# Cross attention: row sums directly behind the product with V in steps 6 and 14, half a V projection ahead of them

## The chip, the core and the metric

The kernel runs on one core of a Trainium2 chip. The metric is the device time of one execution in microseconds (us). Engines, by the names that the profile uses: PE is TensorE (matmuls), PEld its weight loads, DVE is VectorE, ACT is ScalarE, POOL is GpSimd, SP the engine that issues most DMAs. All arithmetic is in 32 bits; an operand of a projection is split into a high and a low part, and a projection is three matmuls.

## The reference

A transformer block on 16 batches of 224 tokens of width 512, with 16 heads of 32, and a context of 750 tokens. The part that matters here is the cross attention:

```
q_c = _ln(x) @ W_qc + b_qc
kv_c = _ln(context) @ W_kvc + b_kvc
k_c, v_c = split(kv_c)                      # B x NH x S x hd
c_attn_w = softmax(einsum(q_c, k_c) * hd ** -0.5)
c_attn_out = einsum(c_attn_w, v_c)
x = x + c_attn_out @ W_cproj + b_cproj
```

Self-attention stands ahead of it, an MLP with gelu behind it. Every batch has the full context.

## The kernel before, in words

Three phases follow each other on all engines: self-attention, cross attention, MLP. The change touches the cross attention alone (`cross_phase`).

There each engine runs a program of its own with `body`, once for each batch b, and in it 16 **steps** h, one for each head. Semaphores alone tie the engines together; the order of the work on each engine is written out by hand. In a step the kernel

- computes the scores of head h+1 with the queries on the partitions (`score`, L1779: unit 0 one matmul of 500 columns, unit 1 one of 500, unit 2 two of 250, into three banks `sc_ps`), from which VectorE takes the row maxima (`row_max`, L1965 and L1967);
- computes the transposed scores of head h-6 (`score_t`, three times two matmuls of 224 columns, L1793, into two banks `tr_ps`), on which ScalarE takes the exponential into `prT` (`exps`, L2138). `score_t` for part c+1 of a head waits until the exponential of the part before the last is done, since there are two banks;
- fills in one or two pieces of the projections for the next batches, by the table `FILL`: `("k", g, half)` and `("v", t)` are twelve matmuls (L72 to L74), of which the first six go between `score_t` 0 and 1 and the last six behind score unit 0; `("c", t)` is four transposes of the normalised context (L1740). They take turns on two banks, even and odd, in the order of `ORDER`, and `bank_free` makes each wait until the last use of its bank is taken out: by ScalarE (`high`) for V, by VectorE (`low`) behind ScalarE for K and c;
- every fourth step, turns the row maxima of four heads (`turn_maxima`, L1767) into the even or odd bank. VectorE splits them (`split_maxima`, L2012 and L2014), and SP places them by DMA beside the queries.

Every fourth step (h = 2, 6, 10, 14) a group of four heads has all its probabilities. Then the product with V (`pv`, L1806, 24 matmuls, four at a time on 32 columns of the array each; the profile has two records for each) and the sums of the probabilities (`sums`, L1815, four matmuls in the same form, of what GpSimd added up in L2211, L2213 and L2215) go into the bank `or_ps`. VectorE inverts the sums (`invert`, L2019) and multiplies (`normalize`, L2025).

In steps 2 and 10 both come at the end of the step. In steps 6 and 14, named by `PV_EARLY`, `FILL` has no projection; there `pv` stands behind `score_t` 0, where otherwise half a projection stands, and `sums` come at the end of the step after, 7 or 15. `divided` gives the step in which VectorE inverts and multiplies: for those groups one step later than for the others. The last batch's groups (`MID_PARTS`, `END_PARTS`) are done piece by piece in another way.

## Time and profile before

| | |
|---|---|
| median of 3 runs | 2614.72 us (2613.72 to 2615.62) |
| the profiled execution | 2619.34 us |
| its span, first to last instruction | 2617.5 us |
| mean granted TensorE clock | 0.991 of full speed |
| busy: PE, DVE, POOL, ACT | 98%, 65%, 49%, 43% of the span |

The profile is of one execution. Its timeline lists instructions of an engine by start, in us from the span's start, with how long each group took; matmuls overlap, so that the distance of two starts and not the duration is what one costs. Like instructions in a row are merged, with their number behind an x. Idle time before an instruction and what ended it stand in brackets.

### The profile page before, as it was taken

Reading aid. Unit: us, or ns where it says so; the run is one execution under the profiler, and the core shown is the slowest. Engines: PE = TensorE matmul, PEld = TensorE weight load, DVE = VectorE, ACT = ScalarE, POOL = GpSimd, SP = SyncE. Lnnn points to the kernel's source line nnn. Section 1 sums busy time; section 2 is a strip of 40 time slices with the busy share of each in tenths; the row PEclk is TensorE's granted clock in tenths of the full one; section 3 lists DMA queues with packets and bytes.
Section 4 is the critical chain, followed back from the end, with each engine's and each line's share of the span. In section 5 each row is a group of like instructions: output and inputs, shape, how many; then the busy total and the mean of one; then the engine's idle time right before and its main releaser. Section 6 shows DMA issues by size and latency. Waiting matters only on the chain.

```text
span 2617.5 us, 50236 instructions
## 1 busy us (share of the span) xinstructions
PE 2578.0 (98%) x18696; PEld 2133.6 (82%) x18696; DVE 1694.1 (65%) x3399; ACT 1126.6 (43%) x2192; POOL 1275.6 (49%) x1426
## 2 busy tenths in 40 slices
PE   8999999999999999999999999999899999999999
PEld 6688888888788888888888888887678888888887
DVE  6677777777757777777777777776764444444442
ACT  4354454444535555555555555554552221212111
POOL 1445455454436777777777777775421121220230
PEclk9999999999899999999999999999899999999999
DMA  8454545555454444444444444434521111111110
GB/s 225 128 136 125 135 120 130 129 129 132 137 148 111 115 115 112 113 114 112 117 114 116 119 113 115 121 90 102 153 94 45 37 44 34 45 49 37 45 53 17
DMA packets 193045, 269.89 MB, mean 103 GB/s; under 512 B 34788, under 2 KB 112612, under 8 KB 192788
## 3 DMA queue, kind: packets, MB, share of 16 engines
q1 hardware_dynamic: 187116, 254.16, 36.9%
q0 software_dynamic: 3264, 7.92, 0.9%
q10 hardware_dynamic: 2424, 4.61, 0.7%
q8 instruction: 150, 2.46, 0.4%
q14 instruction: 91, 0.75, 0.1%
HBM read 111.11 MB, written 36.77 MB: 56 GB/s over the span
## 4 chain that ended last, share of the span: by engine, by line
PE 69%; DVE 1%; issue 0%; DMA 0%; ACT 0%; SPq 0%; DVEq 0%; ACTq 0%
PE late_tr_ps L1793 7%; PE late_sc_ps L1779 7%; PE late_or_ps L1806 5%; PE late_even_ps L72 5%; PE late_sc_ps L72 5%; PE late_even_ps L73 5%; PE late_even_ps L74 5%; PE late_sc_ps L74 5%; PE late_sc_ps L73 5%; PE late_odd_ps L72 3%; PE late_odd_ps L74 3%; PE late_odd_ps L73 3%; PE late_tr_ps L74 2%; PE late_tr_ps L72 2%; PE late_tr_ps L73 2%; PE late_odd_ps L1740 1%
## 5 line engine op out<-in xcount | busy, mean ns | idle before, releaser
L2138 ACT ACTIVATE cross_prT<-late_tr_ps 125x448 f32<-125x448 f32 x759 | 403.0, 544 | 273.5 <-PE late_tr_ps L1793 264.6
L1965 DVE TENSOR_REDUCE cross_parts<-late_sc_ps 112x1 f32<-112x500 f32 x512 | 335.5, 663 | 221.8 <-PE late_sc_ps L1779 220.7
L2211 POOL TENSOR_TENSOR cross_part<-cross_prT 125x448 f32<-125x448 f32 x232 | 271.2, 1169 | 214.6 <-ACT cross_prT L2138 176.9
L1295 POOL TENSOR_TENSOR self_psum<-self_prT 112x224 f32<-112x224 f32 x256 | 179.0, 699 | 328.3 <-ACT self_prT L1160 319.5
L1793 PE MATMUL late_tr_ps<-cross_qst,cross_kst 98*125 98x224 f32 x1536 | 309.5, 284 | 5.4 <-ACT cross_prT L2138 4.4
L1793 PEld LDWEIGHTS late_tr_ps<-cross_qst,cross_kst 98*125 98x125 f32 x1536 | 255.3, 188 | 55.8 <-ACT cross_prT L2138 16.5
L2613 ACT ACTIVATE mlp_hv<-late_sc_ps,mlp_b 128x512 f32<-128x512 f32 x112 | 77.0, 687 | 511.5 <-PE late_sc_ps L74 497.1
L2213 POOL TENSOR_TENSOR cross_part<-cross_part,cross_prT 125x448 f32<-125x448 f32 x232 | 268.5, 1157 | 18.2
L1779 PE MATMUL late_sc_ps<-cross_kst,cross_qst 96*112 96x500 f32 (+1 forms) x1024 | 262.2, 337 | 5.2 <-PEq L99 3.3
L2527 DVE CAST mlp_hT_h<-mlp_hv 128x512 fp32r<-128x512 f32 x112 | 55.9, 499 | 301.8 <-ACT mlp_hv L2613 301.8
L1160 ACT ACTIVATE self_prT<-self_st_ps 112x448 f32<-112x448 f32 x256 | 138.4, 541 | 167.6 <-PE self_st_ps L628 166.4
L1779 PEld LDWEIGHTS late_sc_ps<-cross_kst,cross_qst 96*112 96x112 f32 x1024 | 165.2, 179 | 20.1 <-issue 3.5
L908 DVE TENSOR_REDUCE self_nmax<-self_sc_ps 112x2 f32<-112x448 f32 x256 | 154.5, 614 | 33.3 <-PE self_sc_ps L599 33.2
L72 PE MATMUL late_sc_ps<-mlp_xT_l,mlp_w_h 128*128 128x512 f32 x448 | 175.8, 393 | 0.0
L74 PE MATMUL late_sc_ps<-mlp_xT_h,mlp_w_h 128*128 128x512 f32 x448 | 175.2, 391 | 0.0
L73 PE MATMUL late_sc_ps<-mlp_xT_h,mlp_w_l 128*128 128x512 f32 x448 | 175.0, 391 | 0.0
L1967 DVE TENSOR_REDUCE cross_parts<-late_sc_ps 112x2 f32<-112x500 f32 x256 | 170.2, 665 | 0.0
L2215 POOL TENSOR_TENSOR cross_psum<-cross_part 125x224 f32<-125x224 f32 x232 | 155.6, 671 | 18.2
L1806 PE MATMUL late_or_ps<-cross_prT,cross_vt 125*32 125x224 f32 x2784 | 143.7, 354 | 0.0
L72 PE MATMUL self_pj_ps<-self_xT_l,self_wqkv_h 128*128 128x224 f32 x512 | 140.6, 275 | 2.4 <-DVE self_wm_gates L1009 1.4
L74 PE MATMUL self_pj_ps<-self_xT_h,self_wqkv_h 128*128 128x224 f32 x512 | 140.6, 275 | 0.0
L73 PE MATMUL self_pj_ps<-self_xT_h,self_wqkv_l 128*128 128x224 f32 x512 | 140.3, 274 | 0.0
(343 smaller groups left out, 6870.9 us busy)
## 6 DMA issues: line engine op xcount, KB each, us to landing
cross_kst<-cross_nat_h SPq DMA_DIRECT2D x508, 93.8 KB, 2.2
cross_kst<-cross_nat_l SPq DMA_DIRECT2D x254, 93.8 KB, 2.2
cross_qst<-qc SPq DMA_DIRECT2D x192, 112.0 KB, 2.5
cross_c_in<-in_context SPq DMA_DIRECT2D x78, 224.0 KB
self_kst<-self_nat_h SPq DMA_DIRECT2D x128, 112.0 KB, 2.3
self_qst<-self_natq_h SPq DMA_DIRECT2D x128, 112.0 KB, 3.0
self_x_in<-in_x SPq DMA_DIRECT2D x16, 448.0 KB, 3.8
self_kst<-self_nat_l SPq DMA_DIRECT2D x64, 112.0 KB, 2.2
```

The costliest lines, as they stand in the source:

```text
L72: pe.matmul(out, lhs[0], rhs[1], start=first, stop=False)
L73: pe.matmul(out, lhs[1], rhs[0], start=False, stop=False)
L74: return pe.matmul(out, lhs[0], rhs[0], start=False, stop=last)
L1295: pool.tensor_tensor(psum[:, j], prT[:, j, 0], prT[:, j, 1], ALU.add).then_inc(p_summed, 1)
L1779: last = pe.matmul(sc_ps[u][0:QN, at:at + cn], qst[g][0:TERMS * HD, j, t * QN:(t + 1) * QN], kst[g][j][0:TERMS * HD, c0:c0 + cn], start=Tr ...
L1793: last = pe.matmul(bank(h, c)[0:SN, m * N:(m + 1) * N], kst[g][j][:, kt * SN:(kt + 1) * SN], qst[g][:, j, :], start=True, stop=True)
L1806: last = pe.matmul(or_ps[HD * j:HD * j + HD, 0:N], vt[b.par][:, kt, h * HD:h * HD + HD], prT[:, slot(h), kt], start=kt == 0, stop=kt == ST ...
L1965: dve.tensor_reduce(parts[:, g % 2, j, u, 0:1], sc_ps[u][0:QN, 0:SHALF[0]], AX_X, ALU.max, negate=True).then_inc(maxed, 1)
L1967: dve.tensor_reduce(parts[:, g % 2, j, :, 1], sc_ps[u][0:QN, 0:QT * SHALF[1]].rearrange("p (t k) -> p t k", t=QT), AX_X, ALU.max, negate=T ...
L2138: act.activation(probabilities(b, h)[:, 2 * c:2 * c + 2], bank(h, c)[0:SN, 0:2 * N].rearrange("p (k t) -> p k t", k=2), ACT.Exp).then_inc( ...
L2211: pool.tensor_tensor(part[:], prT[:, j, 0:2], prT[:, j, 2:4], ALU.add).then_inc(pre_summed, 1)
L2213: pool.tensor_tensor(part[:], part[:], prT[:, j, 4:6], ALU.add).then_inc(pre_summed, 1)
```

## The change

`HALF_EARLY` names steps 7 and 15. Their V projection's first half moves to the step before, behind score unit 0 (and a second half, of which these steps have none). `pv` leaves its early place and stands with `sums` at the end of steps 6 and 14, as in 2 and 10. `divided` treats all groups alike, so VectorE inverts and multiplies one step earlier for these. `PV_EARLY` is left to put the transposes `("c", 4)` at the start of step 14.

```diff
+    HALF_EARLY = {7: 6, 15: 14}
...
         for back in (lag - 1, lag):
             step = last_step(b, h - back)
-            if (step < NH and ((h - back) % NH not in PV_EARLY or step >= 0)) == (back == lag - 1):
+            if (step < NH) == (back == lag - 1):
                 found += late_group(b, h - back, att, prv)
...
                 for o, l in late(b, h, att, prv):
                     score_t(o, l, 0)
-                for o, g in late_group(b, h, att, prv) if h in PV_EARLY and steady else ():
-                    pv(o, g)
                 for f, o in fill_at(b, h, "c") if h in PV_EARLY else ():
                     fill_(o, f)
-                for f, o in fill_at(b, h, "kv"):
+                for f, o in fill_at(b, h, "kv") if h not in HALF_EARLY else ():
                     fill_(o, f, (0,))
...
                 for f, o in fill_at(b, h, "kv"):
                     fill_(o, f, (1,))
+                for f, o in fill_at(b, h + 1, "kv") if HALF_EARLY.get(h + 1) == h else ():
+                    fill_(o, f, (0,))
...
-                for o, g in late_group(b, h, att, prv) if h not in PV_EARLY and steady else ():
+                for o, g in late_group(b, h, att, prv) if steady else ():
                     pv(o, g)
                     sums(o, g)
-                for o, g in late_group(b, h - 1, att, prv) if h - 1 in PV_EARLY and steady else ():
-                    sums(o, g)
```

The code below the new line stands one line lower: L1793 is L1794 in the changed kernel, and so on.

TensorE in step 6, before (`tr_ps` is a pair of transposed scores, `sc_ps` scores, `or_ps` the product with V and the sums, `even_ps` and `odd_ps` the banks of the fills; the trio is the last two L1779 rows):

```order
L1793 MATMUL late_tr_ps<-cross_qst_70,cross_kst_68 125x224 x2
L1806 MATMUL late_or_ps<-cross_prT,cross_vt_76 32x224 x24
L1793 MATMUL late_tr_ps<-cross_qst_70,cross_kst_68 125x224 x2
L1779 MATMUL late_sc_ps<-cross_kst_69,cross_qst_71 112x500
L1793 MATMUL late_tr_ps<-cross_qst_70,cross_kst_68 125x224 x2
L1779 MATMUL late_sc_ps<-cross_kst_69,cross_qst_71 112x500
L1779 MATMUL late_sc_ps<-cross_kst_69,cross_qst_71 112x250 x2
L1793 MATMUL late_tr_ps<-cross_qst_70,cross_kst_68 125x224 x2
L72 MATMUL late_even_ps<-cross_wkv_l,cross_cT_h 125x512
```

With the change:

```order
L1794 MATMUL late_tr_ps<-cross_qst_70,cross_kst_68 125x224 x4
L1780 MATMUL late_sc_ps<-cross_kst_69,cross_qst_71 112x500
L72 MATMUL late_even_ps<-cross_wkv_l,cross_cT_h 125x512
...
L1794 MATMUL late_tr_ps<-cross_qst_70,cross_kst_68 125x224 x2
L1780 MATMUL late_sc_ps<-cross_kst_69,cross_qst_71 112x500
L1780 MATMUL late_sc_ps<-cross_kst_69,cross_qst_71 112x250 x2
L1807 MATMUL late_or_ps<-cross_prT,cross_vt_76 32x224 x24
L1816 MATMUL late_or_ps<-cross_psum,cross_ones 32x224 x4
L1794 MATMUL late_tr_ps<-cross_qst_70,cross_kst_68 125x224 x4
```

The product with V went from between the first two pairs to the end of the step, the sums came up behind it from the end of step 7, and six V matmuls (L72 to L74, twice) came up from step 7.

TensorE in step 14, from the transposes that end step 13, before:

```order
L1740 MATMUL late_even_ps<-shared_ident,cross_c_in 128x125 x4
L1793 MATMUL late_tr_ps<-cross_qst_14188,cross_kst_14186 125x224 x2
L1806 MATMUL late_or_ps<-cross_prT,cross_vt_76 32x224 x24
L1740 MATMUL late_odd_ps<-shared_ident,cross_c_in 128x125 x4
L1793 MATMUL late_tr_ps<-cross_qst_14188,cross_kst_14186 125x224 x2
L1779 MATMUL late_sc_ps<-cross_kst_14193,cross_qst_14189 112x500
L1793 MATMUL late_tr_ps<-cross_qst_14188,cross_kst_14186 125x224 x2
L1779 MATMUL late_sc_ps<-cross_kst_14193,cross_qst_14189 112x500
L1779 MATMUL late_sc_ps<-cross_kst_14193,cross_qst_14189 112x250 x2
```

With the change, up to the end of step 14:

```order
L1741 MATMUL late_even_ps<-shared_ident,cross_c_in 128x125 x4
L1794 MATMUL late_tr_ps<-cross_qst_14188,cross_kst_14186 125x224 x2
L1741 MATMUL late_odd_ps<-shared_ident,cross_c_in 128x125 x4
L1794 MATMUL late_tr_ps<-cross_qst_14188,cross_kst_14186 125x224 x2
L1780 MATMUL late_sc_ps<-cross_kst_14193,cross_qst_14189 112x500
L72 MATMUL late_even_ps<-cross_wkv_l,cross_cT_h 125x512
...
L1794 MATMUL late_tr_ps<-cross_qst_14188,cross_kst_14186 125x224 x2
L1780 MATMUL late_sc_ps<-cross_kst_14193,cross_qst_14189 112x500
L1780 MATMUL late_sc_ps<-cross_kst_14193,cross_qst_14189 112x250 x2
L1807 MATMUL late_or_ps<-cross_prT,cross_vt_76 32x224 x24
L1816 MATMUL late_or_ps<-cross_psum,cross_ones 32x224 x4
```

The transposes into `odd_ps` and the pair behind them stand directly behind the first pair, and six matmuls into `even_ps`, last written by the transposes that end step 13, come before the second-to-last pair.

VectorE at the end of step 7 and in step 8, before:

```order
L1965 TENSOR_REDUCE cross_parts<-late_sc_ps 112x1
L1967 TENSOR_REDUCE cross_parts<-late_sc_ps 112x2
L1929 BN_STATS cross_st<-cross_c_in 125x6
L1965 TENSOR_REDUCE cross_parts<-late_sc_ps 112x1 x2
L1967 TENSOR_REDUCE cross_parts<-late_sc_ps 112x2
L1958 SCALAR_TENSOR_TENSOR cross_nat_l<-late_odd_ps,shared_bkv,cross_nat_h 128x376
L2019 RECIPROCAL cross_rb<-late_or_ps 128x224
```

With the change:

```order
L1964 TENSOR_REDUCE cross_parts<-late_sc_ps 112x1
L1966 TENSOR_REDUCE cross_parts<-late_sc_ps 112x2
L2018 RECIPROCAL cross_rb<-late_or_ps 128x224
L1928 BN_STATS cross_st<-cross_c_in 125x6
L1964 TENSOR_REDUCE cross_parts<-late_sc_ps 112x1
L2024 TENSOR_TENSOR cross_ou<-late_or_ps,cross_rb 128x224
L1964 TENSOR_REDUCE cross_parts<-late_sc_ps 112x1
```

The reciprocal moved from behind the row maxima of step 8 and the low part of K to ahead of them.

## Rows read from the trace of the kernel before

**Rows 1.** Stretch: us; busy PE, PEld, DVE, ACT, POOL; PE clock, DMA share, GB/s.

```profile
1298.10:1368.80 70.70, 70.69 (x582) 59.50 (x581) 51.66 (x99) 38.81 (x75) 52.31 (x57) 1.00 0.44 115
```

**Rows 2.** Timeline of TensorE, step 2: start, duration, engine, line, operation, count.

```profile
1341.28 0.63 PE L1779 MATMUL late_sc_ps<-cross_kst,cross_qst 96*112 96x500 f32 x3
1341.83 2.48 PE L1806 MATMUL late_or_ps<-cross_prT,cross_vt 125*32 125x224 f32 x48
1344.13 0.56 PE L1815 MATMUL late_or_ps<-cross_psum,cross_ones 125*32 125x224 f32 x8
1344.62 0.48 PE L1793 MATMUL late_tr_ps<-cross_qst,cross_kst 98*125 98x224 f32 x2
```

**Rows 3.** Timeline of TensorE, steps 6 and 7.

```profile
1355.07 0.38 PE L1793 MATMUL late_tr_ps<-cross_qst,cross_kst 98*125 98x224 f32 x2
1355.41 2.48 PE L1806 MATMUL late_or_ps<-cross_prT,cross_vt 125*32 125x224 f32 x48
...
1358.58 0.62 PE L1779 MATMUL late_sc_ps<-cross_kst,cross_qst 96*112 96x500 f32 x3
1359.03 0.38 PE L1793 MATMUL late_tr_ps<-cross_qst,cross_kst 98*125 98x224 f32 x2
...
1362.48 0.26 PE L1767 MATMUL late_odd_ps<-shared_ident,cross_nmax 112*8 112x112 f32 x1
...
1362.80 0.62 PE L1779 MATMUL late_sc_ps<-cross_kst,cross_qst 96*112 96x500 f32 x3
1363.35 0.58 PE L1815 MATMUL late_or_ps<-cross_psum,cross_ones 125*32 125x224 f32 x8
1363.87 0.48 PE L1793 MATMUL late_tr_ps<-cross_qst,cross_kst 98*125 98x224 f32 x2
1364.18 0.34 PE L72 MATMUL late_odd_ps<-cross_cT_l,cross_wkv_h 128*128 128x376 f32 x1
```

**Rows 4.** Timeline of ScalarE and of GpSimd around step 6.

```profile
1354.81 0.55 ACT L2138 ACTIVATE cross_prT<-late_tr_ps 125x448 f32<-125x448 f32 x1 [0.92 <-PE late_tr_ps L1793]
...
1359.58 0.68 POOL L2215 TENSOR_TENSOR cross_psum<-cross_part 125x224 f32<-125x224 f32 x1
```

**Rows 5.** Timeline of TensorE, steps 14 and 15.

```profile
1321.48 0.46 PE L1793 MATMUL late_tr_ps<-cross_qst,cross_kst 98*125 98x224 f32 x2
1321.86 2.48 PE L1806 MATMUL late_or_ps<-cross_prT,cross_vt 125*32 125x224 f32 x48
1324.27 0.65 PE L1740 MATMUL late_odd_ps<-shared_ident,cross_c_in 125*128 125x125 f32 x4
1324.67 0.46 PE L1793 MATMUL late_tr_ps<-cross_qst,cross_kst 98*125 98x224 f32 x2
...
1325.41 0.61 PE L1779 MATMUL late_sc_ps<-cross_kst,cross_qst 96*112 96x500 f32 x3
1326.03 0.48 PE L1793 MATMUL late_tr_ps<-cross_qst,cross_kst 98*125 98x224 f32 x2
...
1331.40 0.46 PE L1793 MATMUL late_tr_ps<-cross_qst,cross_kst 98*125 98x224 f32 x2
```

**Rows 6.** Timelines of ScalarE and VectorE, steps 13, 14 and 0.

```profile
1321.30 0.58 ACT L2099 COPY cross_vt<-late_odd_ps 125x512 f32<-125x512 f32 x1
...
1325.43 0.55 ACT L2138 ACTIVATE cross_prT<-late_tr_ps 125x448 f32<-125x448 f32 x1
...
1322.39 0.68 DVE L1952 TENSOR_TENSOR cross_cT_l<-late_even_ps,cross_cT_h 128x500 fp32r<-128x500 f32 x1
...
1336.56 1.55 DVE L2019 RECIPROCAL cross_rb<-late_or_ps 128x224 f32<-128x224 f32 x1
```

**Rows 7.** Timelines of TensorE and VectorE, step 11.

```profile
1311.48 0.26 PE L1767 MATMUL late_odd_ps<-shared_ident,cross_nmax 112*8 112x112 f32 x1
...
1312.44 0.62 PE L1740 MATMUL late_odd_ps<-shared_ident,cross_c_in 125*128 125x125 f32 x4
...
1312.08 0.26 DVE L2014 TENSOR_TENSOR cross_mrow_l<-late_odd_ps,cross_mrow_h 8x112 fp32r<-8x112 f32 x1
```

## The prediction

> **What bounds the kernel now.** Read first the busy time by stretch. Over one batch of the cross attention (70.70 us, which repeats from batch to batch) TensorE is busy for 70.69 us at granted clock 1.00, the others for 52 us or less [rows 1]. So the time is the sum of TensorE's own queue, and the busy share hides two kinds of loss in it: a matmul that starts later than its form needs, because the kind of matmul changed, or because it waited for another engine for less than the one before takes to drain. Both show only in start-to-start times, so I read the timeline of TensorE next, and always subtract start from start. The durations printed there overlap; they are not the cost.
>
> Words used below: a pair is the two L1793 matmuls of one score_t; a single is the one 500-column L1779 matmul of a head, a trio the three that follow; turn is L1767; PV is L1806, sums is L1815; c is four L1740 transposes.
>
> **Prices of the pieces.** A trio takes 0.45 us before a pair (1358.58 to 1359.03), but 0.55 before sums or PV; PV takes 2.41 us alone (1321.86 to 1324.27) and 2.30 with sums behind it; sums take 0.52 alone and 0.49 behind PV; the pair behind either takes 0.31 [rows 2, 3, 5]. A single and the pair behind it take 0.43 together: the stretch 1324.67 to 1325.41 is 0.74 and starts with a pair behind transposes, which I price like the one behind sums, 0.31 [rows 3, 5]. Of the 0.43 I give the pair 0.22. From the pair at 1359.03 to the turn at 1362.48 lie pair, half V projection, pair, single, half V projection: 3.45 us, so a half is 1.40; from turn to trio 0.32 [rows 3].
>
> **Term A, steps 6 and 7 (14 batches).** Before, from the first pair of step 6 (1355.07) to the first K product of step 8 (1364.18): 9.11 us [rows 3]. The change takes the PV out from between pair and pair, puts half a projection behind the single, PV and sums behind the trio, and takes sums out of step 7. What becomes late: the second pair of step 6 now stands directly behind the first. It waits for the last exponential of step 5, which ends at 1354.81+0.55=1355.36 [rows 4]. ScalarE to TensorE costs 0.05: an exponential ends at 1325.98, the pair that needs it starts at 1326.03 [rows 5, 6]. So it starts at 1355.41, 0.34 behind the first and not 0.22. A pair released this way takes 0.32 and not 0.22: the one at 1326.03 prints 0.48 for two matmuls where a free one prints 0.38 [rows 3, 5]. Sum: 0.34 + 0.32 + trio 0.55 + PV 2.30 + sums 0.49 + pair 0.31 + the block 3.45 + 0.32 + trio 0.45 + single and pair 0.43 = 8.96. **Gain 0.15 us, 14 times: 2.1.** The last batch with such a PV in its step 14 has no transposes; there nothing gates the second pair, as ScalarE is done with the last exponential before the step (the copy that it starts at 1321.30 stands behind it [rows 6]). Gain 0.15+0.12+0.10=0.37, once.
>
> A rule of the chip would make this better. By the Trainium skill, "TensorE: Matmul & The Clock Gate", section "Step-by-step: what each phase is for", the queue of TensorE loads the next weights while the present matmul runs. If that held for a matmul that waits, the released pair would take 0.22 and the sum would end 1.4 us lower; the row at 1326.03 shows the load was not hidden, so I take 0.32.
>
> **Term B, steps 14 and 15 (14 batches).** Before, from the first pair of step 14 (1321.48) to that of the next step 0 (1331.40): 9.92 us [rows 5]. Part of this is a wait that the change removes: the trio at 1325.41 takes 0.62 and the pair behind it 0.32, because ScalarE sat behind the transposes that stood behind PV. But two waits come in its place.
> First: the half projection of ("v", 5) now comes in step 14, and it shares its bank with the transposes ("c", 3) of step 13; it must wait until VectorE has taken their low part. Unhindered it would stand at 1321.48 + 0.31 + 0.40 + 0.52 = 1322.71. VectorE ends that at 1322.39+0.68=1323.07, and VectorE to TensorE costs 0.10 (L2014 ends at 1312.34, its transposes start at 1312.44) [rows 6, 7]: 1323.17, a wait of 0.46. The transposes ("c", 4) wait for the copy of ("v", 4) too, to 1321.30+0.58=1321.88 [rows 6] instead of 1321.79; this lies inside the 0.46. Queued behind are the pair of step 14, the scores of the next head and PV; no one outside TensorE ends later for it than the order itself makes it.
> Second: without sums between trio and c in step 15, the transposes ("c", 5) come 0.32+0.45=0.77 behind the turn, and they may not start before VectorE has read the turned maxima out of the same bank. Step 11 has just this shape today, and there turn to c is 0.96 [rows 7]. A wait of 0.19.
> From 1323.17: the 3.45 block's pieces + 0.55 + 2.30 + 0.49 + 0.31 = 7.10, turn at 1330.27; plus 0.96, plus c 0.40: 1331.63 against 1331.40. **Loss 0.23 us, 14 times: 3.2.** In step 7 the same turn is followed by 0.32+0.45+0.22=0.99 before the K product, just over 0.96: no wait.
>
> **Edits costed at nothing.** The inversion (1.55 us [rows 6]) and the product on VectorE come one step earlier. The cover is the distance from a row maximum to the score that overwrites its bank, a whole step of 3 us or more. GpSimd: its sum waits for sums only on reuse of the slot; it is released earlier. In step 6 the sums need the last head's probabilities summed by GpSimd, at 1359.58+0.68=1360.26 [rows 4], plus 0.10; they come up at 1355.07+0.66+1.83+0.55+2.30=1360.41. Margin 0.05, taken as enough. No DMA moves in its queue; the maxima's two transfers start about 0.5 us later and are needed three steps on. In the first batch step 6 holds no PV; only the half projection moves, into a step with little in it: taken as zero, it may give some tenths once.
>
> **Sum.** -2.1 - 0.4 + 3.2 = +0.7 us. The profiled execution took 2619.3 us (span 2617.5), 4.6 over the median of the three runs, 2614.7; the terms are differences and apply to either. Predicted: 2615.4 us. 0.2% is 5.2 us, about what a measurement here can tell from no change; both sides of the sum stay under it.
>
> **Rivals.**
> 1. *No gate bites.* The engines ahead finish earlier in the new order, and only the saved changes between 32-column and full-width matmuls count. Then A gives 0.37 fifteen times, 5.5; B ends at 1322.71+7.10+0.77+0.40=1330.98, 0.42 fourteen times, 5.9: 2603.3 us. For it: such losses are 0.1 at each border in the rows. By the Trainium skill, "TensorEngine Tiling (Array Packing)", section "Key Properties", a change of tiling mode drains TensorE; by this rule alone the change gains everywhere. Against: the ends at 1355.36 and 1323.07 hang on instructions that stand ahead of anything moved. Chance 0.05.
> 2. *The wait on the bank of ("c", 3) is shorter or gone*, as VectorE gets to it sooner, the rest as forecast: B becomes 0.23 gain (1322.71+7.10+0.96+0.40=1331.17), sum -5.7: 2609.0 us. With the neighbours of this case (A's gate gone instead: 2612.4) chance 0.14, of which 0.10 ends faster by over 5.2.
> 3. *Slower: sums wait for GpSimd.* The sums of step 6 move ahead by 3 us and stand at the head of TensorE's queue. The margin is 0.05; everything GpSimd ends later than that is paid 14 times, and everything in the queue waits. It decides from 0.32 us a batch beyond the margin; at 0.4 the time is 2615.4+5.6=2621.0. For: GpSimd has a store and an inverse deviation ahead of that head's sums. Against: these start from work that nothing moves. Chance 0.05.
> 4. *Slower: the inversion ahead of three row maxima makes a score wait* in steps 9 and 1. Each 0.2 us would be paid 28 times, 5.6: also 2621. The cover is the step that passes between a maximum and the next score on its bank, against 1.55 of inversion. Chance 0.03.
> 5. *The change does not do what it says*: excluded by the order above for TensorE and VectorE; what remains is in 3.
>
> **Numbers.** Forecast (within 0.2%) 0.73, rivals 1 and 2 as given, 3 and 4 together 0.08. Faster by over 0.2%: 0.15. Slower: 0.08. The same: 0.77. The range takes in the waits being off one at a time (2609.0), and on the other side rival 3 at 0.3 us a batch: 14 x 0.3 = 4.2, 2619.6.
>
> **What would show it.** Batch length 70.70 + 0.23 - 0.15 = 70.8 us. In step 6: second pair 0.34 behind the first, PV and sums 2.79 together, the 9.11 stretch at 8.96. In step 14: the L72 product at 1323.17-1321.48=1.69 behind the first pair, turn to c 0.96 in step 15, and no more 0.62 trio. Wrong if L1815 in step 6 has GpSimd as its releaser, if the first V product stands 1.23 behind that pair, or if the batch length moves by more than 0.3 us.

## The result, and the profile after

| | before | with the change |
|---|---|---|
| median of 16 runs each, same chip | 2616.87 us (2613.72 to 2619.07) | 2620.98 us (2617.50 to 2622.55) |
| ratio, 95% interval | | 1.0016 [1.0009, 1.0024] |
| profiled execution, span | 2617.5 us, mean clock 0.991 | 2619.3 us, mean clock 0.994 |
| busy PE, DVE, POOL, ACT | 98, 65, 49, 43% | 98, 65, 49, 43% |

So the change makes the kernel 4.1 us slower, by an interval that excludes no change, but stays within the 5.2 us that the prediction took as "the same". The forecast was +0.7 us, and its time, 2615.4, lies below every run of the changed kernel; its range ended at 2619.6. Part of that is the baseline: the three runs that the forecast was built on had a median of 2614.72, and the 16 runs beside the changed kernel 2616.87, 2.15 us more. The other 3.4 us are real errors of the sum. Two single executions far above all others, one of the kernel before at 7774 us and one of the kernel e7 at 3588 us, are left out of every figure here. The line numbers of the changed kernel are one or so off those of before: L1794 is the pair, L1780 single and trio, L1768 the turn, L1807 PV, L1816 sums, L1741 the c transposes. The words pair, single, trio, turn, PV, sums and c are those of the prediction; a half is half a V or K projection.

One batch of the cross attention in the changed kernel (stretch, busy PE, PEld, DVE, ACT, POOL, clock, DMA share, GB/s), from the turn of step 11 to that of the next batch's step 11, against [rows 1]:

```profile
1303.57:1374.43 70.86, 70.72 (x588) 59.70 (x584) 51.50 (x100) 38.61 (x74) 52.19 (x57) 1.00 0.44 116
```

The batch repeats at 70.83 to 70.87 us in two executions of the changed kernel; it was 70.70 in all three of the kernel before. TensorE is still the bound and still busy nearly all the time: what was lost hides inside the busy share again, so the start-to-start times have to be read.

Steps 6 and 7, timeline of TensorE, from the first pair of step 6 to the first K product of step 8, against [rows 3]:

```profile
1352.73 0.82 PE L1794 MATMUL late_tr_ps<-cross_qst,cross_kst 98*125 98x224 f32 x4
1353.38 0.40 PE L1780 MATMUL late_sc_ps<-cross_kst,cross_qst 96*112 96x500 f32 x1
...
1355.22 0.62 PE L1780 MATMUL late_sc_ps<-cross_kst,cross_qst 96*112 96x500 f32 x3
1355.77 2.48 PE L1807 MATMUL late_or_ps<-cross_prT,cross_vt 125*32 125x224 f32 x48
1358.07 0.56 PE L1816 MATMUL late_or_ps<-cross_psum,cross_ones 125*32 125x224 f32 x8
1358.56 0.70 PE L1794 MATMUL late_tr_ps<-cross_qst,cross_kst 98*125 98x224 f32 x4
...
1360.71 0.26 PE L1768 MATMUL late_odd_ps<-shared_ident,cross_nmax 112*8 112x112 f32 x1
...
1361.04 0.62 PE L1780 MATMUL late_sc_ps<-cross_kst,cross_qst 96*112 96x500 f32 x3
...
1361.71 0.37 PE L72 MATMUL late_odd_ps<-cross_cT_l,cross_wkv_h 128*128 128x376 f32 x1
```

1361.71-1352.73 is 8.98 where it was 9.11; the forecast was 8.96. The first row holds both pairs of step 6, since nothing stands between them now; the single comes 0.65 behind their start, the 0.34 + 0.32 of the forecast. PV and sums take 1358.56-1355.77=2.79, to the hundredth.

Steps 14 and 15, timeline of TensorE, against [rows 5], and below it the two instructions of VectorE that gate it and the two weight loads of TensorE (PEld) that wait for them:

```profile
1318.88 0.46 PE L1794 MATMUL late_tr_ps<-cross_qst,cross_kst 98*125 98x224 f32 x2
1319.34 0.65 PE L1741 MATMUL late_odd_ps<-shared_ident,cross_c_in 125*128 125x125 f32 x4
...
1320.53 0.49 PE L72 MATMUL late_even_ps<-cross_wkv_l,cross_cT_h 128*125 128x512 f32 x1
...
1322.01 0.38 PE L1794 MATMUL late_tr_ps<-cross_qst,cross_kst 98*125 98x224 f32 x2
1322.23 0.62 PE L1780 MATMUL late_sc_ps<-cross_kst,cross_qst 96*112 96x500 f32 x3
1322.78 2.48 PE L1807 MATMUL late_or_ps<-cross_prT,cross_vt 125*32 125x224 f32 x48
1325.07 0.56 PE L1816 MATMUL late_or_ps<-cross_psum,cross_ones 125*32 125x224 f32 x8
1325.57 0.69 PE L1794 MATMUL late_tr_ps<-cross_qst,cross_kst 98*125 98x224 f32 x4
...
1327.72 0.26 PE L1768 MATMUL late_odd_ps<-shared_ident,cross_nmax 112*8 112x112 f32 x1
...
1328.05 0.62 PE L1780 MATMUL late_sc_ps<-cross_kst,cross_qst 96*112 96x500 f32 x3
1328.68 0.62 PE L1741 MATMUL late_odd_ps<-shared_ident,cross_c_in 125*128 125x125 f32 x4
1329.05 0.35 PE L1794 MATMUL late_tr_ps<-cross_qst,cross_kst 98*125 98x224 f32 x1
```

```profile
1319.80 0.68 DVE L1951 TENSOR_TENSOR cross_cT_l<-late_even_ps,cross_cT_h 128x500 fp32r<-128x500 f32 x1
...
1328.31 0.26 DVE L2013 TENSOR_TENSOR cross_mrow_l<-late_odd_ps,cross_mrow_h 8x112 fp32r<-8x112 f32 x1
...
1320.53 0.18 PEld L72 LDWEIGHTS late_even_ps<-cross_wkv_l,cross_cT_h 128*125 128x125 f32 x1 [0.42 <-DVE cross_cT_l L1951]
...
1328.65 0.41 PEld L1741 LDWEIGHTS late_odd_ps<-shared_ident,cross_c_in 125*128 125x128 f32 x4 [0.19 <-issue]
```

1329.05-1318.88 is 10.17 where it was 9.92; the forecast was 10.15. Both forecast waits are there. The low part of ("c", 3) ends at 1319.80+0.68=1320.48 and the V product on its bank starts at 1320.53, 1.65 behind the first pair (forecast 1.69). From the turn to the last c transposes is 1328.68-1327.72=0.96, and they start 0.11 behind the end of VectorE's split (1328.31+0.26). No matmul row has a bracket with a wait. The starts show the waits, and so do the rows of the weight loads, which name VectorE's L1951 as the releaser of the V product.

So the two main terms were right. What the sum left out is outside them. Times between turns of the row maxima, in us, read from the starts of L1767/L1768 (first batch: from its first turn, 16 steps; last stretch: from step 3 of batch 14, counted from 0, to step 3 of batch 15, the last):

| | before | change | change, second execution | forecast difference |
|---|---|---|---|---|
| first batch | 67.55 | 68.80 | 68.23 | +0.2 |
| the 13 batches that follow | 919.08 | 921.12 | 920.75 | +1.0 |
| last stretch | 63.80 | 66.99 | 65.56 | -0.5 |

The forecast has term B fourteen times, in batches 0 to 13, and term A fourteen times, in batches 1 to 14: so the first row has one B, and the last one A and the extra gain of batch 14.

Most of the last row has a cause that a table by stretch shows. In the changed kernel, batch 15, steps 1 and 2, first by stretch and then TensorE's and VectorE's timelines:

```profile
1824.00:1826.00 2.00, 1.18 (x6) 0.76 (x5) 2.00 (x5) 1.07 (x3) 0.29 (x1) 1.00 0.02 4
1826.00:1828.40 2.40, 2.28 (x8) 1.67 (x8) 2.34 (x4) 1.02 (x3) 0.27 (x1) 0.57 0.51 152
1828.40:1833.20 4.80, 4.80 (x49) 2.17 (x49) 0.68 (x1) 0.41 (x1) 0.00 (x0) 0.50 0.53 143
```

```profile
1825.18 0.48 PE L1780 MATMUL late_sc_ps<-cross_kst,cross_qst 96*112 96x500 f32 x1 [0.69 <-DVE cross_parts L1964]
...
1826.06 1.34 PE L1780 MATMUL late_sc_ps<-cross_kst,cross_qst 96*112 96x500 f32 x3 [0.19 <-DVE cross_parts L1964]
...
1828.56 4.71 PE L1836 MATMUL late_or_ps<-cross_prT,cross_vt 125*32 125x224 f32 x48
...
1823.06 1.53 DVE L2018 RECIPROCAL cross_rb<-late_or_ps 128x224 f32<-128x224 f32 x1
...
1824.52 0.60 DVE L1964 TENSOR_REDUCE cross_parts<-late_sc_ps 112x1 f32<-112x500 f32 x1
```

And in the kernel before the single ahead of the same PV, and the stretch of that PV:

```profile
1828.57 0.48 PE L1779 MATMUL late_sc_ps<-cross_kst,cross_qst 96*112 96x500 f32 x1 [0.68 <-DVE cross_parts L1965]
...
1828.90:1831.40 2.50, 2.50 (x50) 1.48 (x49) 1.66 (x3) 0.00 (x0) 0.56 (x1) 1.00 0.78 209
```

In the last batch no projections are left to fill in, so TensorE waits for VectorE's row maxima: 0.69 us ahead of the single at 1825.18, 0.19 ahead of the trio at 1826.06, and only 1.18 of the 2 us ahead are busy. Within 1.2 us behind the end of the first of these waits the granted clock falls to 0.50, the 1.2 GHz level, and the product with V that follows takes 4.71 us. In the kernel before it ran at 1.00, all its records inside the 2.50 us of the last row.

The waits themselves are not new. The kernel before waits 0.68 us for the same row maxima, one step later, ahead of the single at 1828.57, and the clock stays. In both kernels the long wait stands behind VectorE's inversion (1.53 us at 1823.06 with the change), which is done ahead of the maximum that the single needs (1824.52+0.60=1825.12, the single starts at 1825.18). The change moves the inversion and with it the wait from step 2 to step 1. This is the mechanism of rival 4, in the last batch alone.

In the changed kernel's profiled execution the clock fell less ahead of the cross attention (its first turn of the cross attention is at 780.3 us, 4.7 sooner than before), and so the span is only 1.8 us longer: the mean clock, 0.994 against 0.991, hides the fall.

### The profile page after: what moved, and what is told of

It is laid out like the page before. It is cut to its first block, busy times and chain, and to the rows that moved or that the text cites. A ratio compares the mean times of both kernels' runs of the same rounds, so it can differ in the third digit from the quotient of the medians.

```text
span 2619.3 us, 50236 instructions
## 1 busy us (share of the span) xinstructions
PE 2574.2 (98%) x18696; PEld 2131.6 (81%) x18696; DVE 1693.4 (65%) x3399; ACT 1123.6 (43%) x2192; POOL 1273.4 (49%) x1426
## 4 chain that ended last, share of the span: by engine, by line
PE 67%; DVE 1%; ACT 1%; issue 1%; SPq 1%; DMA 0%; ACTq 0%; DVEq 0%
PE late_tr_ps L1794 7%; PE late_sc_ps L1780 6%; PE late_or_ps L1807 5%; PE late_even_ps L72 5%; PE late_sc_ps L72 5%; PE late_sc_ps L74 5%; PE late_sc_ps L73 5%; PE late_even_ps L74 5%; PE late_even_ps L73 5%; PE late_odd_ps L72 3%; PE late_odd_ps L74 3%; PE late_odd_ps L73 3%; PE late_tr_ps L74 2%; PE late_tr_ps L72 2%; PE late_tr_ps L73 2%; PE late_odd_ps L1741 1%
## 5 line engine op out<-in xcount | busy, mean ns | idle before, releaser
L1794 PE MATMUL late_tr_ps<-cross_qst,cross_kst 98*125 98x224 f32 x1536 | 304.8, 285 | 5.8 <-ACT cross_prT L2137 4.0
L1794 PEld LDWEIGHTS late_tr_ps<-cross_qst,cross_kst 98*125 98x125 f32 x1536 | 251.5, 188 | 54.8 <-issue 21.2
L1780 PE MATMUL late_sc_ps<-cross_kst,cross_qst 96*112 96x500 f32 (+1 forms) x1024 | 262.0, 337 | 5.4 <-PEq L99 3.3
L1780 PEld LDWEIGHTS late_sc_ps<-cross_kst,cross_qst 96*112 96x112 f32 x1024 | 164.5, 178 | 20.3 <-issue 3.4
L72 PE MATMUL late_sc_ps<-mlp_xT_l,mlp_w_h 128*128 128x512 f32 x448 | 175.8, 392 | 0.0
L74 PE MATMUL late_sc_ps<-mlp_xT_h,mlp_w_h 128*128 128x512 f32 x448 | 175.1, 391 | 0.0
L1807 PE MATMUL late_or_ps<-cross_prT,cross_vt 125*32 125x224 f32 x2784 | 143.7, 354 | 0.0
L72 PE MATMUL self_pj_ps<-self_xT_l,self_wqkv_h 128*128 128x224 f32 x512 | 140.7, 275 | 2.4 <-DVE self_wm_gates L1009 1.4
L74 PE MATMUL self_pj_ps<-self_xT_h,self_wqkv_h 128*128 128x224 f32 x512 | 140.6, 275 | 0.0
```

Of the source, the lines that this page charges most:

```text
L72: pe.matmul(out, lhs[0], rhs[1], start=first, stop=False)
L74: return pe.matmul(out, lhs[0], rhs[0], start=False, stop=last)
L1780: last = pe.matmul(sc_ps[u][0:QN, at:at + cn], qst[g][0:TERMS * HD, j, t * QN:(t + 1) * QN], kst[g][j][0:TERMS * HD, c0:c0 + cn], start=Tr ...
L1794: last = pe.matmul(bank(h, c)[0:SN, m * N:(m + 1) * N], kst[g][j][:, kt * SN:(kt + 1) * SN], qst[g][:, j, :], start=True, stop=True)
L1807: last = pe.matmul(or_ps[HD * j:HD * j + HD, 0:N], vt[b.par][:, kt, h * HD:h * HD + HD], prT[:, slot(h), kt], start=kt == 0, stop=kt == ST ...
```

## The experiments

All ratios are to the kernel before, measured in turn on the same chip within a set; there are four sets, on four chips (e1 to e4; e7 and e8; e9 to e12; e13 to e16). The clock is the mean granted clock over the timed runs. A is steps 6/7 and B steps 14/15 as above, medians over the batches of the one profiled execution. "PV" is the first product with V in step 2 of the last batch, from its start to that of the next matmul. For the changed kernel's first execution it is 4.64.

| run | ratio [95%] | clock | A | B | batch | PV | last stretch |
|---|---|---|---|---|---|---|---|
| before, 4 sets | 1 | 0.9939 | 9.11 | 9.92 | 70.70 | 2.41 | 63.80 |
| e1_again | 1.0014 [1.0005, 1.0023] | 0.9934 | 8.98 | 10.19 | 70.83 | 3.98 | 65.56 |
| e2_step6 | 0.9991 [0.9982, 1.0000] | 0.9945 | 8.98 | 9.89 | 70.60 | 4.09 | 65.45 |
| e3_step14 | 1.0023 [1.0014, 1.0032] | 0.9929 | 9.14 | 10.18 | 70.93 | 3.12 | 65.59 |
| e4_late_divide | 1.0009 [1.0000, 1.0018] | 0.9935 | 8.98 | 10.18 | 70.81 | 3.72 | 65.22 |
| e7_swap | 1.0020 [1.0011, 1.0029] | 0.9931 | 9.08 | 10.18 | 70.93 | 4.52 | 66.68 |
| e8_trio | 0.9993 [0.9984, 1.0002] | 0.9929 | 8.98 | 9.81 | 70.45 | 4.29 | 66.93 |
| e9_warm | 1.0012 [1.0003, 1.0021] | 0.9939 | 8.98 | 10.19 | 70.82 | 2.41 | 64.27 |
| e10_turn | 0.9998 [0.9989, 1.0007] | 0.9931 | 9.01 | 9.97 | 70.40 | 4.64 | 68.07* |
| e11_best | 0.9966 [0.9953, 0.9978] | 0.9948 | 9.01 | 9.59 | 70.08 | 2.41 | 65.57* |
| e12_first | 1.0018 [1.0010, 1.0027] | 0.9932 | 8.98 | 10.19 | 70.83 | 2.41 | 63.92 |
| e13_plain | 0.9977 [0.9967, 0.9986] | 0.9929 | 9.01 | 9.59 | 70.08 | 2.41 | 65.24* |
| e14_before_warm | 1.0004 [0.9995, 1.0013] | 0.9935 | 9.11 | 9.92 | 70.70 | 2.41 | 63.97 |
| e15_old_last | 1.0011 [1.0002, 1.0019] | 0.9940 | 8.98 | 10.19 | 70.82 | 2.41 | 63.72 |
| e16_all | 0.9965 [0.9953, 0.9977] | 0.9937 | 9.01 | 9.61 | 70.05 | 2.41 | 65.07* |

(* These start the stretch at a turn that stands 1.02 us earlier, ahead of half a K projection, and end it at one that doesn't: subtract 1.02.)

**The change again, and its two halves.** e1 is the changed kernel, unedited.

> The changed kernel once more, nothing edited. Theory: the slowdown has three parts, 0.167 us in each of 13 steady batches (2.2 us), about 0.7 us once in the first batch (a K product of step 8 waits for VectorE), and about 2.7 us once in the last batch, where the granted clock was 0.50 for some 5 us. If the clock's fall belongs to the new order, it shows again here and the ratio is near 1.0020. Rival: the fall was chance; then the clock reads 1.00 in the last batch this time and the ratio is near 1.0010. The batch length reads 70.87 us either way.

e2 and e3 make one half each, by a table of their own beside `HALF_EARLY` and by `PV_FIRST` in the place of `PV_EARLY` where the diff had struck it (e2; in e3 the two are {15: 14} and (6,)):

```diff
-    HALF_EARLY = {7: 6, 15: 14}
+    HALF_EARLY = {7: 6}
+    PV_FIRST = (14,)
```

> The change in steps 6 and 7 alone; steps 14 and 15 as before. By the step times of the two traces the batch becomes 70.70 - 0.13 = 70.57 us, perhaps 0.05 more from step 8, so 1.7 to 1.1 us less over 13 batches, against 0.7 lost in the first batch. The last batch keeps its sums in step 15 and VectorE its late inversion there, so theory one sees no fall of the clock: ratio 0.9993 to 0.9998. If the two steps act on each other instead, the batch keeps more than 70.7.

> The change in steps 14 and 15 alone; steps 6 and 7 as before. Batch 70.70 + 0.25 = 70.95 us, 3.3 us over 13 batches; no loss in the first batch's step 8. If the fall of the clock in the last batch comes from what steps 14 and 15 leave behind, it shows here too: ratio 1.0022 or so. If it was chance or comes from step 6, 1.0013.

The halves act as forecast and independently: A alone shortens, B alone lengthens. Against 70.70 the batch is 0.10 shorter with the one and 0.23 longer with the other, together 0.13. In time the halves are at 0.9991 and 1.0023, and the sum of the two, 1.0014, is what both together measure. The slower half is 6.0 us where 13 batches of 0.23 are 3.0: more than B is in it. The first batch has one B too (67.86 for 67.55), and the mean clock is 0.0010 lower, worth 1.2 us at the slope found below; the rest was not traced. The fall of the clock came in e3's trace, as forecast, but also in e2's (PV 4.09), where the forecast had none.

**The earlier inversion.** e4 leaves VectorE's inversion and product of these groups where they were.

```diff
-            if (step < NH) == (back == lag - 1):
+            if (step < NH and ((h - back) % NH not in PV_EARLY or step >= 0)) == (back == lag - 1):
```

> The changed kernel with VectorE's inversion and product for the groups of steps 6 and 14 left one step later, as before. If VectorE's earlier inversion is what makes a score of the last batch's step 1 wait (0.69 us) and so lets the clock fall, the clock stays at 1.00 there and some 2.7 us come back: ratio near 1.0008. It would also take back the 0.05 us a batch that steps 6, 7, 14 and 15 don't explain. If the order on TensorE alone does it, nothing changes against the changed kernel: ratio 1.0016.

70.81 against 70.83 and 70.87: at most 0.06 us a batch, and A and B don't move. The ratio falls from 1.0014 to 1.0009, near the 1.0008 that its first theory gave, but each lies inside the other's interval. The trace goes against that theory: the wait of 0.69 us in step 1 is gone, one of 0.74 us stands in step 2 instead, and the clock falls all the same (PV 3.72). So, as far as one trace tells, the place of the inversion decides where the last batch waits and not whether the clock falls, and in the other batches it costs next to nothing.

**The kernel before, twice more,** one execution with a profile each, to see how its trace varies.

> The kernel before once more, for its trace alone. The clock fell in the last batch in the traces of the changed kernel and of its parts alike, in that of the kernel before it didn't. If the fall is chance and the first trace of the kernel before a lucky one, it shows here too: a product of 24 matmuls in step 2 of the last batch takes more than 2.41 us. If it belongs to the change, that product takes 2.41.

> As the run before it, a third trace of the kernel before: chance would show the fall in most traces of either kernel; the theory of the order shows it in none of the kernel before.

They took 2619.97 and 2617.18 us. Batch (70.70), B, and the last stretch (63.80, 63.86) repeat; what varies is the time to the first scores of the cross attention, 769.0 to 771.0 us, where the clock falls at other places from run to run.

**Another order in step 6.** e7 puts the single of the next head ahead of the second pair, to fill its forecast wait for ScalarE.

```diff
+                if h == 6 and att:
+                    score(b, h + 1, 0)
                 for o, l in late(b, h, att, prv):
                     score_t(o, l, 1)
-                if h < NH - 1 and att:
+                if h < NH - 1 and not (h == 6) and att:
                     score(b, h + 1, 0)
```

> The changed kernel, but in step 6 the single score matmul of the next head goes ahead of the second pair, which waits for the last exponential of step 5. If that wait and the bare weight load behind it are the whole of what step 6 loses (0.125 + 0.09 us), the stretch of steps 6 and 7 falls from 8.98 to 8.76 us and the batch from 70.85 to 70.63: ratio to the kernel before 1.0003. If the wait has another source, it moves behind the score and the stretch stays at 8.98.

A miss: A is 9.08, not 8.76, and the batch is 0.06 to 0.10 longer than with the change; the ratio, 1.0020, can't be told from 1.0014 to 1.0016. Timelines of TensorE and VectorE in e7:

```profile
1355.48 0.38 PE L1794 MATMUL late_tr_ps<-cross_qst,cross_kst 98*125 98x224 f32 x2
1355.93 0.49 PE L1780 MATMUL late_sc_ps<-cross_kst,cross_qst 96*112 96x500 f32 x1
1356.26 0.38 PE L1794 MATMUL late_tr_ps<-cross_qst,cross_kst 98*125 98x224 f32 x2
...
1355.23 0.65 DVE L1966 TENSOR_REDUCE cross_parts<-late_sc_ps 112x1 f32<-112x500 f32 x1
```

The single waits too: it overwrites the bank whose maximum VectorE is taking in the reduction that ends at 1355.23+0.65=1355.88, and starts at 1355.93. The single stands 0.45 behind the pair, not 0.22, and then takes 0.33 where a free one takes 0.21. One wait, of 0.12 and 0.10 for the released pair, was exchanged for a longer one, of 0.23 and 0.12 for the released single. The prediction named the bank of the maxima as a cover of a whole step; for the unit that is issued first in a step it isn't.

**Filling the first gate of steps 14/15.** e8 issues the trio ahead of the half V projection in step 14.

```diff
                 if h == NH - 1 and nxt:
                     score(a, 0, 0)
+                for u in (1, 2) if h == 14 and att else ():
+                    score(b, h + 1, u)
```

(and leaves it out at its old place.)

> The changed kernel, but in step 14 the trio of score matmuls goes ahead of the half V projection. If that projection waits 0.46 us for VectorE's copy out of its bank, the trio (0.45) fits into the wait: the stretch of steps 14 and 15 falls from 10.18 to about 9.72 us, the batch from 70.85 to 70.4, ratio 0.9991. If the wait were TensorE's own (a change of matmul form, the queue), the trio would add its time elsewhere and the stretch would stay at 10.2.

Timeline of TensorE in e8:

```profile
1315.13 0.46 PE L1794 MATMUL late_tr_ps<-cross_qst,cross_kst 98*125 98x224 f32 x2
...
1316.28 0.84 PE L1780 MATMUL late_sc_ps<-cross_kst,cross_qst 96*112 96x500 f32 x4
...
1318.65 2.48 PE L1807 MATMUL late_or_ps<-cross_prT,cross_vt 125*32 125x224 f32 x48
...
1323.60 0.26 PE L1768 MATMUL late_odd_ps<-shared_ident,cross_nmax 112*8 112x112 f32 x1
...
1324.56 0.40 PE L1741 MATMUL late_odd_ps<-shared_ident,cross_c_in 125*128 125x125 f32 x2
```

From the first pair to PV 1318.65-1315.13=3.52, against 1322.78-1318.88=3.90 with the change: the wait for VectorE's low part is filled by work, B is 9.81 (forecast 9.72) and less than before the change. The second gate is untouched: turn to c is 1324.56-1323.60=0.96 again. The ratio is 0.0021 to 0.0023 below that of the change, 5.5 to 6 us, where 13 batches of 0.38 to 0.42 give 4.9 to 5.5.

**Removing the second gate.** e10 issues the turn ahead of the second half projection, not behind it.

> The change with the turn of the row maxima ahead of the second half of the V projection, in every step that has one (3, 7, 11, 15), instead of behind it. Theory 1 (the second gate of the forecast: the product with the row maxima in step 15 waits for VectorE's copy of the turn): the 0.19 us of it go, steps 14/15 take 9.99 us instead of 10.18, step 11 loses its 0.17 too, the batch is 70.45 to 70.55 and the ratio 0.999 to 0.9998. Theory 2 (the turn itself then waits for the last row maximum on VectorE, which ends too late for it): the turn waits 0.2 us or more, and the batch stays at 70.8 to 70.9 with a ratio of 1.0014.

Timeline of TensorE in e10:

```profile
1322.84 0.26 PE L1768 MATMUL late_odd_ps<-shared_ident,cross_nmax 112*8 112x112 f32 x1
...
1324.55 0.62 PE L1780 MATMUL late_sc_ps<-cross_kst,cross_qst 96*112 96x500 f32 x3
1325.01 0.38 PE L1741 MATMUL late_odd_ps<-shared_ident,cross_c_in 125*128 125x125 f32 x2
```

Now 2.17 us lie between turn and c, VectorE has long split the maxima, and c follows the trio by 0.46 (it was 0.63). B loses 0.21, and the batch 0.43 to 0.47: it is at 70.40, a little below the forecast 70.45 to 70.55. Steps 3 and 7 have the turn too, and the six K matmuls that stood 1.00 behind it take 1.04 or 1.05 again and not 1.07.

**Keeping TensorE busy in the last batch.** e9 is the change with 16 dummy transposes in the last batch's steps 0 to 2; their output is not used.

```diff
+        WARM = {(0, 0): 2, (1, 1): 8, (1, 2): 3, (2, 1): 3}
+        def warm(b, h, place):
+            if b.c == B - 1 and (h, place) in WARM:
+                pe.wait_ge(m_row, KC * (B - 1))
+                keep_warm(pe, odd_ps, ident, WARM[h, place])
```

> The change as made, with 16 dummy transposes on TensorE in steps 0 to 2 of the last batch alone, where it waits for VectorE's row maxima (2 after the first pair of step 0, 8 ahead of the single of step 1, 3 behind its second pair, 3 in step 2). Nothing else moves, so steps 6/7 stay at 8.98 us, steps 14/15 at 10.18 and the batch at 70.83 to 70.87. Theory 1 (the granted clock falls in step 2 of the last batch because of those waits): the product with V there takes 2.4 us instead of 4.0 to 4.7, from the 14th batch's start to the last turn it is 63.8 to 64.3 us instead of 65.6 to 67.0, and the kernel is at 1.0003 to 1.0008 of the one before (1.0015 without the transposes). Theory 2 (the fall has to do with where the last batch lies in time, or with the whole chip's load, not with those waits): the product keeps 4 us or more and the ratio stays at 1.0014 to 1.0018.

The profile is as theory 1 has it: clock 1.00, PV 2.41, last stretch 64.27. But the traces of e12, e13 and e16, below, have no fall ahead of this PV either, without any transposes, so one such trace decides nothing. The mean clock of the timed runs is 0.9939, that of the kernel before, where the ten kernels with the new steps 14/15 and no transposes have 0.9929 to 0.9937. The mean of eleven runs is itself known to some 0.0004, so this too is a hint at most. And the ratio, 1.0012, is above theory 1's window and as near to the other's: the 0.8 us that the clock is worth (below) is partly paid back, 64.27 against 63.92 in e12.

e14 puts the same transposes into the kernel before.

> The kernel before with the 16 dummy transposes in the last batch, nothing of the change. Theory 1 (the clock's fall in step 2 comes with the change alone): no gain, 0.9998 to 1.0003, mean clock 0.994 as before. Theory 2 (the same waits cost the kernel before as well, in some of its runs): 0.9990 to 0.9996 with a mean clock of 0.995.

No gain: 1.0004, just above theory 1's window, with a mean clock of 0.9935 against 0.9937 of the kernel before in the same set. Where the clock didn't fall there was nothing to be had.

**Where the fall comes from.** e12 keeps steps 6/7 of the first batch as before; in the text on record the batches are counted a batch short: there are 16.

> The change as made except in steps 6/7 of the first of the 15 batches, which keep the order of before. Theory 1 (in the first batch the earlier half projection makes the K product of step 8 come before VectorE has split its tile): from the turn of step 7 to the K product is 1.00 us instead of 1.65 there, and the kernel is 0.3 to 0.65 us shorter than the change, a ratio of 1.0013. Theory 2 (the wait only moves): the same time as the change, 1.0015. The clock's fall in the last batch should be there in either case, with 65.5 to 67.0 us from the 14th batch's start to the last turn; should it be gone, the fall is not tied to the steps of the last batch but to what lies 1.8 ms ahead or to chance.

e15 keeps the old order in steps 14/15 of batch 14 alone, the ones ahead of the last batch.

> The change as made, except that steps 14/15 of the 14th of the 15 batches, the ones right ahead of the last batch, keep the order of before. Theory 1 (what those steps leave VectorE brings the waits that let the clock fall in step 2 of the last batch): the product with V there takes 2.4 us, the mean clock of the timed runs is 0.994 and the ratio 1.0005 to 1.0010. Theory 2 (chance, or any shift of the last batch against the clock's own steps): the product with V may take 4 us in the profile, the mean clock is 0.993 and the ratio 1.0013 to 1.0016.

First e12. The K product of step 8 of the first batch comes 1.00 us behind the turn again and the first batch takes 67.82, against 68.23 to 68.80, so what the change does there is shown in the trace. What is left above the 67.55 of the kernel before is the one B of this batch (e3, with steps 6/7 as before, has 67.86); e14, whose first batch is that of the kernel before, took 67.93, so a few tenths are also chance. The rows of the changed kernel, TensorE and VectorE:

```profile
793.25 0.26 PE L1768 MATMUL late_odd_ps<-shared_ident,cross_nmax 112*8 112x112 f32 x1
...
794.04 0.38 PE L1794 MATMUL late_tr_ps<-cross_qst,cross_kst 98*125 98x224 f32 x2
794.90 0.41 PE L72 MATMUL late_odd_ps<-cross_cT_l,cross_wkv_h 128*128 128x376 f32 x1 [0.49 <-issue]
...
792.92 0.82 DVE L1941 SCALAR_TENSOR_TENSOR cross_nm<-cross_mv,cross_rs 125x3 f32<-125x3 f32 x1
...
794.54 0.26 DVE L2013 TENSOR_TENSOR cross_mrow_l<-late_odd_ps,cross_mrow_h 8x112 fp32r<-8x112 f32 x1
```

The K product at 794.90, 1.65 behind the turn, starts 0.10 behind VectorE's L2013, which ends at 794.80 and takes the turned maxima out of that bank. VectorE is late because it first does L1941, 0.82 us, and a row maximum. In the timed runs the 0.4 to 1.0 us are not seen: 1.0018 is no better than 1.0014 to 1.0016. And the fall in the last batch is absent in e12's profile though its last batch is that of the change: the fall is no fixed cost, it comes in some executions. The waits in e12's last batch are those of the changed kernel to 0.01 us (0.69 and 0.19), and the clock stays at 1.00 behind them. Where the fall is absent, the last stretch is 63.92.

Counted over all traces without transposes, the clock falls between the last batch's first wait and the end of its first PV in seven of ten with the new steps 14/15 ahead (the changed kernel, e1, e3, e4, e7, e8, e10, but not e12, e13, e16), and in one of five with the old (e2, but not e15 nor the three of the kernel before). In every trace but that of e15, with the change and without, it falls again 4.5 to 6.7 us behind the end of the last stretch.

In e15 the clock stays at 1.00 through this whole stretch, PV takes its 2.41 (from 1827.22 on), and the next 5 us read:

```profile
1828.00:1833.00 5.00, 5.00 (x90) 3.13 (x82) 2.23 (x5) 0.54 (x1) 0.00 (x0) 1.00 0.61 154
```

Its mean clock is 0.9940 and its ratio 1.0011, as theory 1 says, though the upper end of its window (1.0010) is just missed and the intervals of 1.0011 and 1.0014 overlap. By the count above, this trace alone decides nothing. The clocks of all timed runs together speak for theory 1: 0.9932 over the 106 runs of the ten kernels that have the new steps 14/15 ahead of the last batch and no transposes (standard error 0.0001), 0.9939 over 106 runs of the kernel before (0.0001), 0.9940 in e15 and 0.9945 in e2, which have the old steps there. Within a kernel, runs with a clock lower by 0.001 are 1.2 us longer (a line through all timed runs, each kernel about its own mean). So the difference of 0.0007 is worth 0.8 us; the mean clock is that of the whole run, and that the 0.0007 arise in the last batch is read from the traces alone. Against it stands one trace: e2's, where the clock fell at the same place under the old order. The order changes how often it falls, as far as these runs tell; what makes it fall in a given execution is open.

**Adding up what gains.** e11 is e8 and e10 together, with the first batch of e12 and the transposes of e9; e13 is e11 without the transposes; e16 is e13 with the late inversion of e4.

> The change in steps 6/7 and, in steps 14/15, with the rest of the scores of step 15 ahead of the half V projection; the turn ahead of the second half; the first batch's steps 6/7 as before; and the dummy transposes in the last batch. If the parts add up: steps 6/7 8.98 us, steps 14/15 9.6 to 9.8, step 11 0.17 less, the batch 70.1 to 70.3, and with the clock kept in the last batch a ratio of 0.9965 to 0.998. If the turn's gain and that of the scores are the same 0.2 us seen twice, the batch stays at 70.3 to 70.45 and the ratio at 0.998 to 0.9993.

> The previous best (steps 6/7 as changed but not in the first batch; in steps 14/15 the rest of the scores ahead of the half V projection; the turn ahead of the second half) without the dummy transposes. Theory 1 (they keep the clock): the batch stays at 70.08 us, the mean granted clock of the timed runs falls from 0.995 to 0.993, and the kernel is at 0.9972 to 0.9980. Theory 2 (they do nothing for the time): 0.9962 to 0.9968, the batch being 0.62 us shorter than before over 13 batches (8.1 us).

> As the version without the transposes, and VectorE's inversion and product of steps 6 and 14 left one step later, as before the change. If the late inversion gives back the 0.04 us a batch that it gave alone: batch 70.0 to 70.05 us and 0.5 us less than the version without it (0.0002, below what the timed runs can tell). If the two are in each other's way: batch 70.1 or more.

One batch of e16:

```profile
1297.97:1368.02 70.05, 70.05 (x588) 59.68 (x584) 51.62 (x99) 38.44 (x74) 52.29 (x57) 1.00 0.45 118
```

The parts add up: 0.38 to 0.42 a batch from e8 and 0.43 to 0.47 from e10, 0.06 to 0.1 less than their sum, give 70.08 and with the late inversion 70.05. With 0.9965 [0.9953, 0.9977] e16 is the best version, some 9 us faster than the kernel before and 13 faster than the change; e11 is level with it. That e13 is at 0.9977 with the same batch as e11 goes with the clock, 0.9929 against 0.9948, 2.3 us at the slope above; whether the transposes do that or chance can't be told from five and nine runs, and e16, without transposes, is level with e11. Its last stretch is 0.17 shorter than that of e13: there the late inversion takes away the wait in step 1 of the last batch.

## Why the prediction was off

- **Term A: right.** 8.98 for 8.96 us, with each piece where it was put. The rule of the Trainium skill, "TensorE: Matmul & The Clock Gate", section "Step-by-step: what each phase is for", that the next weights load while a matmul runs, would have given 8.86 here. The trace speaks against it for a matmul that waits on a semaphore: the released pair again took 0.10 more, and the V product released at 1320.53, whose six take 1.48 where the free ones at 1326.33 take 1.39, lost 0.09. The weight load at 1320.53, above, shows why: it starts with its matmul and not ahead of it.
- **Term B: right.** 10.17 to 10.19 for 10.15. Both gates were named with place and size; e8 and e10 remove one each, and B falls by 0.37 and 0.21.
- **Edits costed at nothing.** The step "in the first batch: taken as zero" was wrong: +0.7 to +1.25 us in the traces where one B, +0.2, was due (e12 brings it back to +0.3, which is that B). The pieces that the change moves fill step 6 there, but the K product of step 8 loses the distance to the turn. The prediction looked at this wait in the steady batches (0.99 against 0.96) and not for the one batch in which no sums or PV stand in between and VectorE has other work. GpSimd never was the releaser (rival 3), and the inversion costs no more than 0.06 a batch (rival 4), save for the wait that it moves in the last batch.
- **The gain of 0.37 in batch 14: wrong sign.** In the last stretch e12 and e15 differ there alone, 63.92 against 63.72: +0.2. Two steps failed. "There nothing gates the second pair, as ScalarE is done with the last exponential before the step" was read from a steady batch, where four transposes delay the step. In batch 14 they are absent, and the exponential ends at 1812.87+0.54=1813.41, behind the start of the first pair; pairs to single is 0.65 again, as in step 6:

```profile
1813.13 0.81 PE L1794 MATMUL late_tr_ps<-cross_qst,cross_kst 98*125 98x224 f32 x4
1813.78 0.39 PE L1780 MATMUL late_sc_ps<-cross_kst,cross_qst 96*112 96x500 f32 x1
...
1812.87 0.54 ACT L2137 ACTIVATE cross_prT<-late_tr_ps 125x448 f32<-125x448 f32 x1 [1.27 <-PE late_tr_ps L1794]
```

  So from the first pair of step 14 to that of the next step 0 it is 8.75 for 8.80, 0.05 less. And what follows, steps 0 to 2 of the last batch, is set by ScalarE's exponentials and VectorE's maxima: it takes 0.25 longer, with the wait for VectorE now in step 1 and not in step 2. A gain ahead of a stretch that another engine bounds is no gain.
- **Not in the sum at all: the clock.** The sum was made from rows at clock 1.00. Behind the last batch's waits it fell in more of the traces with the change, and the mean clock of the timed runs is lower by 0.0007, which goes with 0.8 us. That the change causes it is likely by these numbers and not shown by an experiment: e9 and e15, made for it, each leave chance open.
- **Together:** 13 batches +1.7 to 2.0 (forecast +1.0: A and B were each off by 0.02 or so; 0.03 more lies in step 8, where the six K matmuls, now 1.00 behind the turn, take 1.07 for 1.04), first batch +0.7 (forecast +0.2), batch 14 and the last +0.1 (forecast -0.5), clock +0.8 (forecast nothing): 3.3 to 3.6 us. The two sets of timed runs gave +4.1, and +2.8 by the medians of e1 or 3.7 by its ratio.
- **The failed step,** then, is "Sum": the first batch's extra wait (0.5), the gain of batch 14 (0.6 too good), the released K product of step 8 and the clock (0.8) were set to zero or below, each by a sentence or by rows of another batch, and all came out above. The two terms that nearly cancel had been worked out to 0.02 us and left a sum smaller than what was left out. The range went by one wait at a time and had no term for the spread of the baseline, whose median of three was 2.15 us low.

## What to carry to other kernels

When two large terms cancel, the sum is set by the edges: the first and the last pass of the loop need rows of their own, since there the cover of the steady state is absent and another engine may be the bound. A product moved one step ahead lands on a bank whose last user is now one step nearer; put work without that wait (here the trio) between, and issue what another engine must answer (the turn) ahead of a long block and not behind it. These two moves, with the first batch left as before, turned 0.16% slower into 0.23% faster (e13); with the late inversion it is 0.35% (e16), the difference between these two being mostly clock and chance.

## What was not expected of the hardware

- A fall of the granted clock to 0.50 that comes during or within 2.5 us behind a wait of 0.5 to 0.74 us, in some executions and not in others of the same instructions (changed kernel: yes; e12, which is the same from the second batch on: no), and makes one product with V take 4.7 us for 2.4. The profile's mean clock (0.994 there, 0.991 before) doesn't tell of it.
- The start of the cross attention, from the first scores to the first turn, takes 12.8 to 12.9 or 13.7 to 14.2 us, by how long the clock is low there. It was the longer one in the three traces of the unedited kernel before and the shorter in e14, and both occur among the kernels with the change. The stretch behind the last turn takes 724.5 or 725.9 us in the same way (in the long ones the clock falls 5.5 to 6 us behind that turn). Single executions differ by this alone by over 1 us, as much as the effect studied.
